# Expert 1's down projection, features first, in float32r products, with a block transposition through DMA and VectorE, and new places for several steps in the queues of an attention and expert kernel

## The reference, cut to what matters

```python
xn = _layernorm(x)
# attention: queries, keys, values of width 32
scores = einsum('btc,bsc->bts', xn @ q_w, xn @ k_w) * decay_weights
att = (einsum('bts,bsc->btc', scores, xn @ v_w) @ o_w.T) * out_scale
# four experts of xn; two are picked per token, weighted by a softmax of their logits
e0 = silu(xn @ sw_w1) * (xn @ sw_w3) @ sw_w2
sym = ((xn @ me_eq_w + me_eq_b) @ me_wv + me_bv) @ me_wo + me_bo
e1 = gelu(sym @ me_c1w + me_c1b) @ me_c2w + me_c2b
h2 = layer_norm(syn + attn)                      # syn, attn: linear in xn
e2 = layer_norm(h2 + relu(h2 @ ce_f1w + b) @ ce_f2w + b) @ ce_gen_w + b
e3 = gelu(xn @ ml_w1 + ml_b1) @ ml_w2 + ml_b2
out = x + att + sum(rw * picked)
```

## Time and profile before

| | us | share of the span |
|---|---|---|
| median of three runs | 455.88 | |
| the profiled execution | 456.09 | |
| its span | 454.2 | |
| PE busy | 442.8 | 97% |
| DVE busy | 404.1 | 89% |
| ACT busy | 269.5 | 59% |
| POOL busy | 249.8 | 55% |
| a group in the middle, 204.00 to 231.04 | 27.04 | PE busy throughout |

### The profile page before, as it was taken

How to read it: one execution, slowest core, us unless ns; L and a number is a source line. 1 busy time by engine, 2 the same in 40 slices (tenths; PEclk the granted TensorE clock), 3 DMA queues, 4 the chain that set the end, 5 groups by cost and what they waited for, 6 DMA issues and landing times.

```text
span 454.2 us, 9552 instructions
## 1 busy us (share of the span) xinstructions
PE 442.8 (97%) x2788; PEld 369.0 (81%) x2788; DVE 404.1 (89%) x1327; ACT 269.5 (59%) x534; POOL 249.8 (55%) x366
## 2 busy tenths in 40 slices
PE   4999999999999999999999999999999999999996
PEld 3778788888878878888888878878888888878776
DVE  5788989989999899999989999999999989997897
ACT  4864828467383855838476482845738385582840
POOL 3883727557273574727557372665727457371461
PEclk9999999999999999999999999999999999999999
DMA  7522123031222303123041222303122140311101
GB/s 264 31 71 71 24 71 69 25 99 42 63 55 64 74 23 92 23 75 64 23 109 30 71 45 69 69 23 93 39 66 56 44 95 23 92 23 48 26 0 48
DMA packets 86483, 27.18 MB, mean 60 GB/s; under 512 B 64992, under 2 KB 82112, under 8 KB 86464
## 3 DMA queue, kind: packets, MB, share of 16 engines
q1 hardware_dynamic: 86176, 26.94, 24.8%
q10 hardware_dynamic: 288, 0.01, 0.0%
HBM read 14.66 MB, written 12.06 MB: 59 GB/s over the span
## 4 chain that ended last, share of the span: by engine, by line
PE 89%; DVE 5%; ACT 3%; issue 1%; DMA 1%; DVEq 0%; SPq 0%
PE S L1116 13%; PE S L1118 12%; PE S L1117 12%; PE EX L1042 12%; PE EX L1062 6%; PE EX L1070 4%; PE S L1204 3%; PE S L1200 3%; PE S L1199 3%; PE ATT L1188 3%; PE S L1131 2%; PE ATT L1227 2%; PE S L1130 2%; PE S L1129 2%; PE TR L1156 2%; PE S L1212 1%
## 5 line engine op out<-in xcount | busy, mean ns | idle before, releaser
L1116 PE MATMUL S<-xh,WH 128*128 128x512 f32 x224 | 98.8, 441 | 0.2 <-DVE gate L805 0.2
L1118 PE MATMUL S<-xh,WL 128*128 128x512 f32 x224 | 88.6, 396 | 0.0
L1117 PE MATMUL S<-xl,WH 128*128 128x512 f32 x224 | 88.2, 394 | 0.0
L482 POOL TENSOR_TENSOR hid3l<-hid,hid3h 128x512 fp32r<-128x512 f32 x64 | 80.3, 1283 | 0.0
L440 POOL TENSOR_TENSOR veps_x<-mv_x,eps 128x4 f32<-128x4 f32 x16 | 3.2, 199 | 120.2 <-DVE mv_x L637 120.2
L615 ACT ACTIVATE hid<-S,me_b 128x512 f32<-128x512 f32 x32 | 22.0, 687 | 61.6 <-PE S L1118 61.3
L1042 PEld LDWEIGHTS EX<-scaled,hid 128*128 128x128 f32 x480 | 55.8, 192 | 2.3 <-issue 1.1
L1042 PE MATMUL EX<-scaled,hid 128*128 128x128 f32 x480 | 56.1, 275 | 0.7 <-DVE me_b L731 0.7
L1116 PEld LDWEIGHTS S<-xh,WH 128*128 128x128 f32 x224 | 42.2, 189 | 17.2 <-issue 3.6
L805 DVE SCALAR_TENSOR_TENSOR gate<-th,S 128x512 f32<-128x512 f32 x64 | 43.9, 687 | 8.1 <-ACT th L561 7.3
L1117 PEld LDWEIGHTS S<-xl,WH 128*128 128x128 f32 x224 | 42.3, 189 | 10.2 <-issue 3.6
(11 more groups left out here) (194 smaller groups left out, 1070.7 us busy)
## 6 DMA issues: line engine op xcount, KB each, us to landing
X<-x SPq DMA_DIRECT2D x16, 256.0 KB, 2.8
turning<-xn SPq DMA_DIRECT2D x15, 256.0 KB, 2.0
xb<-turning SPq DMA_DIRECT2D x60, 64.0 KB, 2.5
turning<-e3T SPq DMA_DIRECT2D x15, 256.0 KB, 2.4
e3b<-turning SPq DMA_DIRECT2D x60, 64.0 KB, 2.5
out<-OUT SPq DMA_DIRECT2D x15, 256.0 KB, 2.4
W<-weights SPq DMA_DIRECT2D x1, 768.0 KB, 8.2
W<-weights SPq DMA_DIRECT2D x1, 512.0 KB, 5.8
```

Source lines behind the costliest of these rows:

```text
L482: pool.tensor_tensor(hid3l[:, j, :], hid[3][:, j, :], hid3h[:, j, :], ALU.subtract) \
L1116: pe.matmul(bank[:, :], wh, hi, start=True, stop=False)
L1117: pe.matmul(bank[:, :], wh, lo, start=False, stop=False)
L1118: pe.matmul(bank[:, :], wl, hi, start=False, stop=True).then_inc(unit_ready, 1)
```

## The change

Expert 1's down projection of groups 0 to 14 becomes what expert 3's is: ACT copies the high parts `hid1h` (two copies, placed between k's copies and `kd`), POOL subtracts the low parts `hid1l` (two, between the root of u and `hid3l`), PE adds six float32r products of 128x512, ACT copies the result with the bias `c2b` into `e1T`, SP sends it through DRAM, and DVE transposes it into `e1t`. The bias is no longer added by DVE to `OUT` with four instructions per group. The last group keeps the old form. The third weight split takes expert 1's `me_c2w` with it (1024 columns in place of 768). In `UNITS` `st` and `sc` change places, so `st` is in bank 2 behind c0, and `sc` in bank 3 behind c1.

Orders that change: on PE `st`, the transpositions of `n1` and `sc` in place of `sc`, transpositions, `st`; expert 2's product in front of the attention's and expert 1's behind them; m0 and m1 in front of expert 0's down projection; the folding of the weights in group 0 at later places. On ACT the tanh of a2 in front of `hidh`, and m's Gelus and the copy of x in front of `e3T`. On DVE the moments of u, expert 0's share and the transposition of e3 in front of the masked scores; the shares of experts 3 and 1 behind the last gates; `u` in front of expert 2's share.

```diff
@@ lists
-UNITS = ["tok0", "tok1", "tok2", "tok3", "a0", "b0", "c0", "c1", "c2", "c3", "sc", "st",
+UNITS = ["tok0", "tok1", "tok2", "tok3", "a0", "b0", "c0", "c1", "c2", "c3", "st", "sc",
-WEIGHT_SPLITS = [(SPLIT["w1"], "sw_w1", 2 * I), (SPLIT["ml"], "ml_w1", I + 2 * P), (SPLIT["f2"], "f2w", 2 * P + I)]
+WEIGHT_SPLITS = [(SPLIT["w1"], "sw_w1", 2 * I), (SPLIT["ml"], "ml_w1", I + 2 * P), (SPLIT["f2"], "f2w", 2 * P + I + 2 * P)]
...
@@ SP
+            at = ROWS["me_c2b"][0]
+            sp.dma_start(c2b[:, :], bass.AP(rows.tensor, rows.offset + at, [[1, P], [1, 1]])).then_inc(c2b_loaded, DMA_INC)
...
+            def swap_e1(g):
+                sp.wait_ge(e1_taken, g.count(1, 1))
+                swap(g, e1b, e1T, turning[2], e1_kept, e1_swapped)
...
                 if not last:
                     swap_x(g.next())
+                if not first:
+                    swap_e1(g.prev())
@@ POOL, behind root_u
+                if not first:
+                    for j in range(2):
+                        pool.wait_ge(hid1_high, g.prev().count(2, j + 1))
+                        pool.tensor_tensor(hid1l[:, j, :], hid[1][:, j, :], hid1h[:, j, :], ALU.subtract) \
+                            .then_inc(hid1_low, 1)
@@ ACT, behind k's copies
+                if not first:
+                    before = g.prev()
+                    for j in range(2):
+                        act.wait_ge(released[before.bank(f"m{j}")], before.uses_before(f"m{j}") + 1)
+                        act.copy(hid1h[:, j, :], hid[1][:, j, :]).then_inc(hid1_high, 1)
@@ ACT, behind hid3h
+                if not first:
+                    act.wait_ge(e1_summed, g.prev().count(1, 1))
+                    wait(act, ex_ready[1], g.prev().count(1, 0))
+                    act.activation(e1T[:, :, :], EX[EX_BANK[1]][:, :, :], ACT.Identity, bias=c2b[:, :]).then_inc(e1_taken, 1)
@@ ACT, later
+                half_gate(2)
                 act.wait_ge(released[g.bank("f1_1")], g.uses_before("f1_1") + 1)
                 act.copy(hidh[:, :, :], hid[2][:, :, :]).then_inc(hid_high, 1)
...
-                half_gate(2)
                 half_gate(3)
+                for j in range(2):
+                    m, free = unit(f"m{j}")
+                    act.activation(hid[1][:, j, :], m[:, :], ACT.Gelu, bias=me_b[:, j:j + 1]).then_inc(free, 1)
+                if not last:
+                    take_x(g.next())
                 wait(act, ex_ready[3], g.count(1, 0))
...
@@ DVE, the end of a group
-                if not first and not last:
+                silu(3)
+                if not first:
+                    mix(g.prev(), 3, ex_taken[0], src=e3t)
+                if first:
                     turn_next(g)
...
+                if not first:
+                    dve.wait_ge(e1_swapped, g.prev().count(SWAPS * DMA_INC, SWAPS * DMA_INC))
+                    dve.transpose(e1t[:, :, :].rearrange("p t n -> p (t n)"), e1b[:, :, :].rearrange("p t n -> p (t n)")) \
+                        .then_inc(ex_ready[1], 1)
...
+                    expert1(g.prev())
+                if not first and not last:
+                    turn_next(g)
@@ PE, expert1
-                for t in range(NT):
-                    for j in range(2):
-                        ins = pe.matmul(EX[EX_BANK[1]][:, t, :], hid[1][:, j, t * P:(t + 1) * P],
-                                        w("me_c2w", j * P, P), start=(j == 0), stop=(j == 1))
-                ins.then_inc(ex_ready[1], 1)
+                for j in range(2):
+                    pe.wait_ge(hid1_high, g.count(2, j + 1))
+                    wh, wl = (m[:, SPLIT["c2"] + j * P:SPLIT["c2"] + (j + 1) * P] for m in (WH, WL))
+                    pe.matmul(bank, wh, hid1h[:, j, :], start=(j == 0), stop=False)
+                    pe.matmul(bank, wl, hid1h[:, j, :], start=False, stop=False)
+                for j in range(2):
+                    pe.wait_ge(hid1_low, g.count(2, j + 1))
+                    wh = WH[:, SPLIT["c2"] + j * P:SPLIT["c2"] + (j + 1) * P]
+                    ins = pe.matmul(bank, wh, hid1l[:, j, :], start=False, stop=(j == 1))
+                ins.then_inc(e1_summed, 1)
```

More of the change, by code:

```diff
@@ L190, in build @@
         hid3l = sb("hid3l", [P, 4, T], F32R)
+        hid1h = sb("hid1h", [P, 2, T], F32R)
+        hid1l = sb("hid1l", [P, 2, T], F32R)
+        e1T = sb("e1T", [P, NT, P])
+        e1b = sb("e1b", [P, NT, P])
+        e1t = sb("e1t", [P, NT, P])
+        c2b = sb("c2b", [P, 1])
         e3T = sb("e3T", [P, NT, P])
@@ L610, in turn @@
                 act.activation(e3T[:, :, :].rearrange("p t n -> p (t n)"), e3[:, :], ACT.Identity, bias=vec("ml_b2")).then_inc(free, 1)
-                if not last:
-                    take_x(g.next())
-                for j in range(2):
-                    m, free = unit(f"m{j}")
-                    act.activation(hid[1][:, j, :], m[:, :], ACT.Gelu, bias=me_b[:, j:j + 1]).then_inc(free, 1)
             turns(act, turn, lambda g: None)
@@ L909, in turn @@
                                          op0=ALU.add, op1=ALU.add).then_inc(free, 1)
-                dve.wait_ge(att_added, g.count(1, 1))
-                for t in range(NT):
-                    ins = dve.scalar_tensor_tensor(out=OUT[g.par][:, t, :], in0=row("me_c2b"),
-                                                   scalar=coef[g.par][:, t, 1:2], in1=OUT[g.par][:, t, :],
-                                                   op0=ALU.mult, op1=ALU.add)
-                ins.then_inc(bias1_added, 1)
-                if first:
-                    turn_next(g)
+                if last:
+                    dve.wait_ge(att_added, g.count(1, 1))
+                    for t in range(NT):
+                        ins = dve.scalar_tensor_tensor(out=OUT[g.par][:, t, :], in0=row("me_c2b"),
+                                                       scalar=coef[g.par][:, t, 1:2], in1=OUT[g.par][:, t, :],
+                                                       op0=ALU.mult, op1=ALU.add)
+                    ins.then_inc(bias1_added, 1)
+                if not first:
+                    expert2_add(g.prev())
                 if not last:
@@ L1147, in turn @@
                     three(f"c{j}", SPLIT["ml"] + j * P, h, l)
+                pe.wait_ge(kd_ready, g.count(1, 1))
+                bank = fill("st")
+                for n in range(BEHIND):
+                    ins = pe.matmul(bank[n * C:(n + 1) * C, 0:C], kd[:, n, :], kv[:, n + 1, C:2 * C],
+                                    start=True, stop=True)
+                ins.then_inc(unit_ready, 1)
+                for t in range(NT):
+                    pe.wait_ge(c_normed, g.count(NT, t + 1))
+                    ins = pe.transpose(TR[:, t * P:(t + 1) * P], n1[:, t, :], ident[:, :])
+                ins.then_inc(c_turned, 1)
+                if first:
+                    fold_first()
                 pe.wait_ge(qk_split, g.count(1, 1))
@@ L1213, in turn @@
                 ins.then_inc(unit_ready, 1)
+                if first:
+                    pe.wait_ge(setup_took, len(TAKEN))
+                three("m0", SPLIT["me"], h, l)
+                three("m1", SPLIT["me"] + P, h, l)
                 if not last:
```

82 lines of the change are left out of this document (33 added, 49 removed).

## The result

The changed kernel took 460.23 us (median of four runs, 459.31 to 462.45) against 455.89 for the kernel before: 1.0085 of its time, with a 95% interval from 1.0056 to 1.0115. Run again beside other kernels it took 461.08 (eight runs, 459.35 to 465.07), 1.0107 with an interval from 1.0072 to 1.0142. It is slower by about 1%, and 460.5 was forecast.

The account below looks back on a forecast made before the run. PE, busy 27.04 us of a 27.04 us group, was taken as the bound. Gain 0.38 and loss 0.69 give +0.31 per group, +4.6 over fifteen; with the ends at 0, 456.09 becomes 460.7, or 460.5 as median; range 453 to 475.

Parts of the forecast that it names:

- PE's gain: On PE, fifteen times: expert 1's float32 products of 1.78 us become six float32r products of 1.40, 0.38 less per group.
- PE's loss: At `st` behind c3: two copies before ACT's Gelus delay c0's bank, so PE stands still 0.69 us per group.
- The sum: PE's time per group, gain 0.38 against loss 0.69: +0.31 us, bound 0.15 either side; fifteen groups give +4.6.
- The ends: Group 0's wait for m's folded bias shrinks about 0.5 us; last group's e3T is 0.4 to 0.5 late; they cancel.
- DVE, POOL, SP: Work added off PE, including expert 1's 6.4 us way through DRAM, stays hidden and costs nothing.
- Rival one: On PE: the queue shortens and `st` isn't held, so the gain comes without the wait: 450.4 us; chance 0.08.
- Rival two: At `h2l`: POOL runs through hid3l without a gap, f1_0 is 4.1 us late; 522, or 465 to 480; chance 0.14.
- Rival three: On DVE: no slack left, so 0.4 us more of collision adds about that much per group: 467; chance 0.13.

Follow-up runs that it names:

- e1t: Not a run: the tile into which DVE transposes expert 1's result after its way through DRAM, in the changed kernel.
- e3T: Not a run: a tile of expert 3's that ACT copies, in the changed kernel behind m's two Gelus.

## Why the prediction was right

**PE's gain, forecast 0.38.** With the copies out of the way the period is 26.61, against 27.04: 0.43. The six products take 1.50 from start to start (245.47 to 246.97), not 1.40, since the first follows float32 products and takes 0.33 to the next; in exchange f1_0's first product, which now follows float32r ones, takes 0.23 to the next and not 0.31. The stretch that holds both, from expert 1's or expert 2's first product to the second of f1_0, is 3.68 before and 3.32 with the copies moved: 0.36. Another 0.05 comes between c3's last product and the second of `gates(1)` (1.74 and 1.69), where `st` and `sc` changed places, and 0.02 in the rest of the group. The bound of 0.1 to either side held.

**PE's loss, forecast 0.69.** The changed kernel's period less that of the kernel with the copies moved is 27.32 - 26.61 = 0.71. Its parts moved against each other: the semaphore and PE's start took 0.14 and not 0.08, while `st` would have begun only 0.32 and not 0.23 behind c3's last product. That makes a wait of 0.98 - 0.32 = 0.66; the other 0.05 are not accounted for by a wait that the trace names. The 0.69 is thus partly luck: the way from ACT to PE was too short by 0.06, the start of `st` too early by 0.09. That the copies are the cause, and not the new place of `st`, is shown from both sides: adding them to the kernel before costs 0.80 per group, and taking `st` back to its place saves nothing.

**The sum, forecast +0.31 per group.** It was +0.27, and 3.8 for fourteen groups where I had 4.6 for fifteen.

**The ends, forecast to cancel.** In the undisturbed profile group 0 is 0.76 shorter (I took 0.5, with a bound of 0.66 that it passed by 0.1; the folds now stand at other places) and the tail some 0.3 longer (0.4 to 0.5). They sum to -0.4, not 0. The execution of that profile took 459.37 in place of the 460.7 that I had worked out. The median stands higher, at 460.23; a late start of PE, as in the first profile, would do that, but the executions without a profile don't show it. So the agreement of 460.2 with 460.5 is better than the working deserves by about 1 us: that much of it is luck.

**DVE, POOL, SP, forecast hidden.** They are. `e1T`'s write is issued at 247.96 and the last of its four reads ends its issue at 252.57, and DVE's transposition at 255.33 has no idle time before it.

**Rival one (450.4)** is what the kernel with the copies moved does, 451.02. The change would have been a gain of 1% had the wait not come with it.

**Rival two (`h2l` shut out, 522)** got 0.14, and its mechanism did not exist in these groups. The measured time can't judge it, since `h2l` would have come in by my count too; the kernels with the copies at the end and with `hid3h`'s first part earlier do. I had taken from `coef` in group 0 that POOL doesn't let DVE in between two of its instructions, and so the whole price hung on a gap of 0.02 us. What I counted right is the collision: `h2l` with 1.70 where I said 1.8, ending 0.55 behind `hid1l`. What I had wrong is the condition. In groups 1 to 15 every `h2l` and every short instruction that met a subtraction came in at the first boundary. The records of `h2l` have a median of 1.71 us in the four kernels with the changed kernel's order and 1.10 in the three with the copies at the end and `h2l` alone, and it ended 0.55 behind the subtraction that it met, whether POOL's next followed at once or after a gap. One row of one group was read as a rule.

**Rival three (DVE the bound)** got 0.13 at "no slack left"; the slack was 0.46, and the added transposition of 0.71 used it up in nearly every group. The count was near, 0.5 us off in 27, though what went beyond the slack was paid only in part.

The Trainium skill (SBUF — State Buffer, "Who interferes with whom") says that whichever engine issues first holds the port for its whole instruction. The runs agree for one instruction: an `h2l` that met a subtraction ended 0.55 behind it. The rule does not say who comes next at a boundary, and there the runs decide: DVE's waiting instruction, and in the one kernel where a second stood behind it that one too, except in group 0.

## What to carry to other kernels

An engine with much idle time can still be the one that PE waits for: before a step is put into its queue, look up what behind it releases PE's next bank, and how much earlier than needed it comes. Here that was 0.3 us at the Gelus (0.44 from the first one's end to `sc`, less the 0.14 of the way to PE) and, in the changed kernel, nothing at `state`; what copies in front of either took beyond that went into the time. Work on tiles that lie ready from the group before belongs where the queue is idle, which here turned a loss of 1% into a gain of 1%.

## What the runs showed of the hardware that I had not expected

A DVE instruction with two SBUF inputs that is issued during a POOL subtraction of 1.28 us starts at the next boundary between two POOL instructions, even if POOL has the next one ready and whether or not a semaphore wait stands between: `h2l` with 1.10 in place of 0.67, in groups 1 to 15. A second DVE instruction directly behind it keeps the access: `small` with 0.59 and `h2l` with 0.68, and POOL's waiting subtraction takes the delay, 1.84 in place of 1.28 (1.75 behind `h2l` alone). In group 0 alone, in four kernels, such an instruction waited through one or two boundaries (2.23 to 3.20 us). The cause of that is open. And PE's first products begin with twice the step from one to the next (0.21 in place of 0.11), with a granted clock of 1.00 in the row of that stretch, and the profiles differ in when that ends, from 9.2 to some 18 us; ten of these products took 2.23 in place of 1.23. Why the row does not show it is open as well.
